# Attention with layer norm on one core: what TensorE does between two bursts of scores

## What is computed

```
q, k, v = x @ wq + bq, x @ wk + bk, x @ wv + bv       # 8 heads of 64
scores  = q @ k.T / 8 + bias[manhattan distance]      # 900 x 900 per head
ctx     = softmax(scores) @ v
out     = layernorm(ctx @ wo + bo + x) * gamma + beta
```

## Time and profile before

| | before |
|---|---|
| median of 3 runs | 3212.4 us (3210.62 to 3213.43) |
| the profiled execution, its own time | 3212.19 us |
| its span, first to last instruction | 3210.2 us |
| mean granted clock of TensorE | 0.993 |
| busy share: TensorE, VectorE, ScalarE, GpSimd | 97%, 81%, 85%, 50% |

### The profile page before, as it was taken

How to read it: one execution, slowest core, us unless ns; L and a number is a source line. 1 busy time by engine, 2 the same in 40 slices (tenths; PEclk the granted TensorE clock), 3 DMA queues, 4 the chain that set the end, 5 groups by cost and what they waited for, 6 DMA issues and landing times. The chain is left out here.

```text
span 3210.2 us, 126640 instructions
## 1 busy us (share of the span) xinstructions
PE 3098.7 (97%) x52264; PEld 2079.8 (65%) x52264; DVE 2610.0 (81%) x5594; ACT 2713.9 (85%) x6903; POOL 1603.4 (50%) x3277
## 2 busy tenths in 40 slices
PE   8899999999999999999999999999999999999986
PEld 5566666666666666666666666666666666666655
DVE  3878879798797978879788797977969788797887
ACT  4988888888888888898888988888888988888885
POOL 1346445465554645546454454645536455464544
PEclk9999999999999999999999999999999999999998
DMA  7332423324233342423324233242332424333231
GB/s 199 73 84 73 94 70 91 77 73 105 62 92 87 76 96 65 96 80 82 85 76 92 71 89 82 73 97 67 95 86 70 98 66 91 86 75 92 65 79 28
DMA packets 523289, 267.80 MB, mean 83 GB/s; under 512 B 329274, under 2 KB 460346, under 8 KB 522590
## 3 DMA queue, kind: packets, MB, share of 16 engines
q1 hardware_dynamic: 375479, 127.82, 18.2%
q10 hardware_dynamic: 147232, 131.88, 14.0%
HBM read 194.10 MB, written 63.44 MB: 80 GB/s over the span
## 5 line engine op out<-in xcount | busy, mean ns | idle before, releaser
L1000 DVE CUSTOM_DVE_ANT_0 prob<-s_ps,window 128x450 f32<-128x450 f32 x1920 | 1107.9, 613 | 441.4 <-PE s_ps L720 441.3
L842 ACT ACTIVATE prob<-prob,own 128x450 f32<-128x450 f32 x1920 | 1265.4, 662 | 142.7 <-DVE own L1000 129.3
L858 ACT ACTIVATE prob<-prob,weight 128x450 f32<-128x450 f32 x1920 | 1173.5, 660 | 47.0 <-POOL weight L1147 44.1
L1016 DVE STREAM_TRANSPOSE prob_t<-prob 128x960 f32<-128x960 f32 x960 | 1125.8, 1173 | 72.7 <-PE pv_ps L740 39.9
L740 PEld LDWEIGHTS pv_ps<-prob_t,values 64*64 64x64 f32 x30720 | 753.6, 133 | 378.0 <-issue 330.9
L720 PE MATMUL s_ps<-k_sb,q_sb 64*32 64x450 f32 x15360 | 853.2, 546 | 38.1 <-DVE own L1000 34.3
L740 PE MATMUL pv_ps<-prob_t,values 64*64 64x120 f32 x30720 | 857.8, 260 | 24.4 <-ACT ctx_sb L868 21.5
L634 PE MATMUL r_ps<-xt,w_sb 128*128 128x450 f32 x3072 | 704.1, 376 | 8.8 <-ACT prob_t L816 3.7
L634 PEld LDWEIGHTS r_ps<-xt,w_sb 128*128 128x128 f32 x3072 | 564.4, 190 | 92.5 <-issue 27.2
L1133 POOL TENSOR_TENSOR lead<-own,other 128x4 f32<-128x4 f32 x480 | 102.1, 213 | 985.0 <-DMA other<-own 984.7
L1147 POOL TENSOR_TENSOR weight<-total,minus_one 128x4 f32<-128x4 f32 x480 | 502.8, 1048 | 37.7
(11 more groups left out here) (63 smaller groups left out, 1488.0 us busy)
## 6 DMA issues: line engine op xcount, KB each, us to landing
w_sb<-w_split ACTq DMA_DIRECT2D x126, 512.0 KB, 4.0
values<-v_dram ACTq DMA_DIRECT2D x256, 240.0 KB, 3.2
other<-own SPq DMA_DIRECT2D x1920, 1.0 KB, 2.2
tokens<-in_x SPq DMA_DIRECT2D x420, 64.0 KB, 3.1
tokens<-in_x SPq DMA_DIRECT2D x109, 240.0 KB, 3.1
out<-tokens SPq DMA_DIRECT2D x105, 240.0 KB, 2.7
v_dram<-stage SPq DMA_DIRECT2D x90, 240.0 KB, 2.8
v_dram<-stage SPq DMA_DIRECT2D x30, 180.0 KB, 2.3
```

Source lines behind the costliest of these rows:

```text
L842: nc.scalar.activation(prob[:, im.unit(u) % RING, head, 0:HALF], prob[:, im.unit(u) % RING, head, 0:HALF], ACT.Exp, scale=-1.0, bias=own[: ...
L858: nc.scalar.activation(prob[:, im.unit(u) % RING, head, 0:HALF], prob[:, im.unit(u) % RING, head, 0:HALF], ACT.Copy, scale=weight[:, s, c: ...
L1000: nc.vector.tensor_tensor_reduce(prob[:, im.unit(u) % RING, head, 0:HALF], s_ps[:, u % 2, head, 0:HALF], window[:, w0:w0 + HALF // GRID, : ...
L1016: nc.vector.transpose(out=prob_t[:, g % 2, v % PER_GROUP, :, :].rearrange("p h k -> p (h k)"), in_=prob[:, im.unit(u) % RING, :, :].rearra ...
```

## The change

Groups have 5 units (three per pair, 12 per image), the ring has 7 units, and a slot holds either one whole group of P x V or up to two whole projections, by a table written out. `x_turned`, the buffer of the transposed new x, lies over a part of `ctx_sb` (the end of pair 2 and the begin of pair 3), which adds two waits to VectorE and one to ScalarE. Eviction times, load times, split times and the order at SyncE change with it.

```diff
-PER_GROUP = 4
+PER_GROUP = 5
-RING = 8
+RING = 7
-PV_UNITS = [4, 8, 12, 16, 20, 24, 28, 32, 34, 38, 42, 46, 50, 54, 58, 62]
-PV_CUT = 8
-SPLIT_UNITS = [0, 0, 4, 6, 8, 11, 14, 17]
-LOAD_X = [22, 24, 28, 32]
+PV_UNITS = [6, 10, 16, 20, 26, 30, 36, 40, 46, 50, 56, 60]
+SPLIT_UNITS = [0, 0, 3, 5, 6, 10, 13, 15]
+LOAD_X = [20, 22, 26, 29]
+X_UNITS = [30, 31, 32, 33, 34, 36, 38, 40]
-FINAL_UNITS = [54, 54, 58, 58, 60, 60, 62, 62]
-FINAL_EVICT = [57, 57, 61, 61, 63, 63, 65, 66]
+FINAL_UNITS = [54, 54, 58, 58, 60, 62, 62, 64]
+FINAL_EVICT = [57, 57, 61, 61, 62, 64, 65, 66]
+def pv_groups(u, last=False):
+    return [g for g, at in enumerate(PV_UNITS) if (min(at, UNITS) if last else at) == u]
+GAPS = {2: pieces(1, (3,)) + [out(0)], 4: [out(1), out(2)], 8: [out(3)] + pieces(2, (0,)), 12: [out(4)] + pieces(2, (1,)),
+        14: [out(5)] + pieces(2, (2,)), 18: [out(6)] + pieces(2, (3,)), 22: [out(7)] + pieces(3, (0,)),
+        24: pieces(3, (1, 2)), 28: pieces(3, (3,)), 32: [value(0), value(1)], 34: [value(2), value(3)],
+        38: [value(4), value(5)], 42: [value(6)] + pieces(4, (0,)), 44: pieces(4, (1, 2)), 48: pieces(4, (3,)),
+        52: [value(7)] + pieces(5, (0,)), 54: pieces(5, (1,)), 58: pieces(5, (2,))}
+SEQUENCE = [item for u in sorted(GAPS) for item in GAPS[u]]
+EVICT = {item: u + (2 if n and item[0] != "out" else 1) for u in GAPS for n, item in enumerate(GAPS[u])}
...
-        x_turned = sb("x_turned", [128, 2, D])
+        x_turned = ctx_flat[:, (PAIRS - 1) * S - 300:(PAIRS - 1) * S - 300 + 2 * D].rearrange("p (i d) -> p i d", i=2)
...
             def body(im, u):                                   (SyncE)
+                for work in im.evicted(u):
+                    if work[0] == "value":
+                        keep_value(im, work[1])
                 if u % 2 and im.live(u + 5):
                     exchange(im, u + 5)
...
-                for work in im.evicted(u - 1):
-                    if work[0] == "value":
-                        keep_value(im, work[1])
...
-                for of, g, j0, j1 in im.parts(u):              (TensorE)
-                    context(of, g, j0, j1)
+                for of, g in im.groups(u):
+                    context(of, g)
                 for work in im.background(u):
-                    work_on(im, work[:-2], *work[-2:])
+                    work_on(im, work)
...
                 if p == 0 and not im.first:                    (ScalarE, keep_context)
-                    act.wait_ge(split_lo, NT * (im.b - 1) + 2 * gi + 2)
+                    act.wait_ge(split_lo, NT * (im.b - 1) + tiles_to(gi))
+                if g == GROUPS - PAIR_GROUPS - 1 and not im.last:
+                    act.wait_ge(x_lo, X_TILES * (im.b + 1))
...
+                if t == 0 and im.first:                        (VectorE, turn_x)
+                    dve.wait_ge(wq_kept, 16 * 2 * PAIRS)
+                elif t == 0:
+                    dve.wait_ge(split_lo, NT * im.b)
...
-                    if X_UNITS[t] - 2 == u and not im.last:    (VectorE, body)
+                    if X_UNITS[t] - 1 == u and not im.last:
```

More of the change, by code:

```diff
@@ L115 @@
 X_TILES = -(-S // XB)
[L116 to L119, removed]
 BANK = {item: n % 2 for n, item in enumerate(SEQUENCE)}
@@ L144, in background @@
 def background(u, first, last):
-    work = [(*item, k0, k1) for item, k0, k1 in STEPS.get(u, []) if wanted(item, first, last)]
+    work = [item for item in GAPS.get(u, []) if wanted(item, first, last)]
     if last:
-        work += [("final", t, 0, KT) for t in range(NT) if FINAL_UNITS[t] == u]
+        work += [("final", t) for t in range(NT) if FINAL_UNITS[t] == u]
     return work
 def order(first, last):
-    return [w[:-2] for u in range(END) for w in background(u, first, last) if w[-1] == steps(w)]
+    return [w for u in range(END) for w in background(u, first, last)]
 def evicted(u, first, last):
@@ L205, in live, with groups @@
         return not (self.first and u < 0) and not (self.last and u >= UNITS)
-    def parts(self, u):
-        before = [] if self.first else [(Before(self), *part) for part in pv_parts(u + UNITS)]
-        return before + [(self, *part) for part in pv_parts(u, self.last) if u < UNITS or self.last]
+    def groups(self, u):
+        before = [] if self.first else [(Before(self), g) for g in pv_groups(u + UNITS)]
+        return before + [(self, g) for g in pv_groups(u, self.last) if u < UNITS or self.last]
     def background(self, u):
@@ L619, in piece @@
                 bank, pair = bank_of(use), im.pair(p)
[L620 to L632, removed]
+                bank_wait(im, use)
+                if im is pro and j == 0:
+                    first_xt_ready(NT - 2)
+                    first_xt_ready(NT - 1)
+                if j == 0 and p == PAIRS and im is not pro:
+                    pe.wait_ge(x_lo, X_TILES * (im.b + 1))
+                if half == 0:
+                    if known(pair):
+                        pe.wait_ge(lo_done[("wk0", "wq0")[kind]], 1)
+                    else:
+                        pe.wait_ge(w_in[kind], 16 * pair)
+                for k in range(KT):
                     for i, (a, c) in enumerate(TERMS):
@@ L694, in work_on @@
                 else:
-                    out_tile(im, work, k0, k1)
+                    out_tile(im, work)
             def scores(im, u):
@@ L914, in body @@
                         stage_value(im, work[1])
-                for of, g, j0, j1 in im.parts(u - 1):
-                    if j1 == BLOCKS:
-                        keep_context(of, g)
+                for of, g in im.groups(u - 1):
+                    keep_context(of, g)
                 if im.live(u + AHEAD):
@@ L1083, in body @@
                 for t in range(X_TILES):
-                    if X_UNITS[t] - 2 == u and not im.last:
+                    if X_UNITS[t] - 1 == u and not im.last:
                         turn_x(im, t)
```

85 lines of the change are left out of this document (36 added, 49 removed).

## The result

| | before | after |
|---|---|---|
| median of 4 runs each | 3212.6 us | 3174.8 us (3168.8 to 3182.1) |
| ratio | | 0.9884 (95% interval 0.9863 to 0.9905) |
| the profiled execution, its own time; its span | 3212.19; 3210.2 | 3174.42; 3172.5 |
| mean granted clock | 0.993 | 0.991 |

What follows compares the result with a forecast made beforehand. TensorE's queue was taken to bound 14 middle images; scores 50.1, P x V 47.8, projections 87.0 and stalls 4.5 us give 189.4 us an image, 5.6 less; 15 x 5.6 = 84 gives 3128 us, range 3095 to 3185.

Steps and rivals of the forecast that it cites:

- Term 1: TensorE's P x V: twelve whole groups of 5 at 3.98 us, 47.8 us per image for 51.1, gain 3.3 us.
- term 2: TensorE's projections merged into 18 slots: 87.0 us per image for 89.4, gain 2.4 us.
- Rival 3: TensorE pays the 0.2 us at every tile shape change, so gains shrink to near nothing: 3205 to 3215 us; chance 0.04.
- Rival 5: TensorE pays a price per key block, at most 0.015 us, saved by 60 fewer blocks: 3114 us; chance 0.02.
- term 3: TensorE's stalls per middle image: 4.5 us after the change, about what stood before (4.4 us).
- SyncE, "I leave 1.5 us": Five loads and three exchanges crowd SyncE's bodies 29 to 33; late exchanges hold ScalarE: 1.5 us of stalls per image.
- The value writes, "nothing, 0.6 us": Value writes moved ahead of SyncE's exchange cost nothing, or their 0.6 us of issue if ScalarE is late.
- `pv_ps`, "1.4 us per image": TensorE's wait for ScalarE to empty this PSUM goes, 1.4 us per image, as groups come at least 4 units apart.
- "1 for what I can't see": Allowance of 1 us of unseen stalls per image, added to 3.5 us of listed ones.
- Rival 1: Uneven slot lengths give thinner covers for ScalarE, adding 3.5 us of stalls per image: 3181 us; chance 0.20.
- Rival 4: TensorE's stalls almost vanish, 1.5 us per image: 3083 us; chance 0.06.
- Rival 2: ScalarE blocks 1.5 us on each whole P x V group, 7.7 us more per image: 3327 us, slower; chance 0.08.

Runs made afterwards that it cites:

- experiment 1: The changed kernel with each tile of new x loaded by one DMA in place of four (tile order differs, values wrong): 3118.5 us.
- experiment 5: The changed kernel with tiles 4 to 7 of the new x loaded in bodies 30, 32, 34, 36 in place of 30 to 33: 3135.9 us.
- experiment 7: The kernel before the change with each tile of new x loaded by one DMA in place of four: 3186.1 us, ratio 0.9918.
- the small norm: The changed kernel with VectorE's statistics, centring and scaling of an output tile over 64 of 512 columns: 3139.8 us.
- experiment 2: The changed kernel with loads of x tiles 3 to 7 at units 28, 30, 32, 34, 36 in place of 29 to 33: 3186.4 us.

## Why the prediction was half right

**Term 1 (P x V) and term 2 (projections) hold.** 3.99 us per group for 3.98, mixed pair 5.42 for 5.4, value pair 5.76 (slot 38: 7.43 less 1.67) for 5.71, two pieces 5.09 for 5.1. Slots without waits sum to 185.3 us for my 184.9 (its 43.4 for eight mixed pairs at 5.4 should be 43.2). The price per burst and column is thus right at 150 columns too, and 60 fewer blocks per image brought no more than that: the 15 blocks of a group take 3.75 us for their columns, and 0.24 is left. By the prediction's estimate, the weight-load rule of the Trainium skill (TensorE: Matmul & The Clock Gate, What overlaps and what doesn't) would have put some 0.2 us into every block, 3 us into a group. This trace disagrees, as the one before did, with its 0.24 us in 15 blocks. Rival 3 falls: the price per burst is 0.24 and not above 0.4. Rival 5 falls too, since the slots without waits sum to more than my figure and not to less. From start to start, no joint between scores and projection costs anything: a burst of scores that nothing delays takes 1.67 us ahead of either.

**The step that failed is term 3, the stalls after:** 4.5 us predicted, 7.8 measured (185.3 to 193.1). A middle image was to fall by 5.6 us and fell by 2.5, 44 us of the missing 46 over the 14: 3.3 an image are these stalls and 0.4 is work, less 0.5 because the mean image before took 195.5 and not the 195.0 of my window. Point by point:

- *SyncE, "I leave 1.5 us".* This is the mis-sized term: by experiment 1 it is 3.5 us (3.8 by the medians), 2.8 of them by the place of the loads alone (experiment 5). I had the right queue in the right bodies, but took 0.6 us per DMA from an exchange, where the loads of the crowded bodies average 0.67 to 0.76, so 21.9 us for 19.4; and I priced the exchange's lateness, not the value write's and not that of the load itself, for which slot 34 waits.
- *The value writes, "nothing, 0.6 us".* Wrong twice. They stand behind whatever loads are still being issued (5.4 us of them in the trace), and ScalarE blocks on them. Moved back, they cost 7.0 us more in a middle image.
- *I set after's loads against nothing:* experiment 7 shows that 2.0 us of the same cost stood in the kernel before, inside my 4.4. What the change added is 1.5.
- *VectorE, "1 us".* 1.7 by the table (2.3 by the medians), but the kernel before had 2.6 of it. The balance of these two is about -0.9, which I did not count.
- *`pv_ps`, "1.4 us per image".* The wait is gone as said, but the earlier trace rows was misread: 10.8 of the 21.5 us lie in the last image, and the 14 middle intervals had 0.6 us each.
- *ScalarE in the singles, "1 us".* Slots 48, 54 and 58 exceed 4.33 by 0.2 us together. Its slack was enough.
- *Ring of 7, `x_turned`.* The ring shows as five waits of VectorE for its own turn, 2.5 us in the whole run; no new wait for `x_turned` shows. A ring of 8 beside groups of five was not run.
- *"1 for what I can't see"* had to hold slot 4, 1.7 us, where a P x V-free pair of output tiles waits for GpSimd's split and ScalarE's eviction at once. In the kernel before slot 4 is 6.46 us and waits for nothing.

The sum of the changes: SyncE +1.5, VectorE -0.9, slot 4 +1.7, the rest (slots 0 and 32, where nothing was tested) +0.6: 2.9, the growth from 4.9 to 7.8. The shares overlap a little, since the causes were taken away one at a time. Slot 4 has the largest of them and stood in no point of my list.

**Ends:** the two half images were to save 5.6 us, with nothing within 5 for the tail; begin and end together saved 3.2.

**Rivals.** Rival 1's time (3181) is nearest, 6 us off, but not by its mechanism. Its sign was scores split by waits in slots 48 to 60 or 6 to 10. The first are the cleanest. Slot 8 does show it (0.9 us an image), but for VectorE, and the small norm takes it away; ScalarE's waits at `ratios` fell from 114.7 to 94.0 us over the span. The stalls sit in the double slots, where two evictions, splits or writes of a kind fall due at once. Rival 4 (3083, stalls of 1.5 us an image) falls with the 7.8. Rival 2 falls: ScalarE waits 45.5 us in all for P x V, 0.24 per group, where it asked for 1.5:

```profile
ACT ratio L811 <- POOL lead L1102: 94.0, 97, 3.6
...
ACT ctx_sb L831 <- PE pv_ps L702: 45.5, 36, 7.5
```

**Open:** what slot 4 would cost with its pair taken apart, how much of slot 32 (0.5 us, GpSimd's split of the new x) is SyncE's, and whether issue or packets hold slot 34.

## What to carry to other kernels

When work is merged into larger bursts, price the burst from start to start, but then list for each helper queue what falls due together: pairs of tiles make pairs of evictions, writes and splits, and a double buffer is full at the third. On a strict queue count every issued DMA of the crowded bodies and ask what short write stands behind them. And take the suspected cost out of the kernel before as well: a cost that both share explains nothing of the difference, however large it is.

## What the runs showed of the hardware

A wait of TensorE can cost more than its length. The windows of experiment 2 around the 3.25 us wait in slot 32 (length, busy time of each engine, granted clock, DMA):

```profile
1516.00:1525.60 9.60, 9.60 (x188) 6.52 (x172) 9.04 (x19) 7.59 (x20) 3.71 (x7) 1.00 0.39 98
1525.60:1528.90 3.30, 0.11 (x1) 0.10 (x1) 0.11 (x1) 2.09 (x6) 2.41 (x5) 1.00 0.46 71
1528.90:1533.10 4.20, 4.14 (x12) 2.75 (x12) 3.48 (x7) 3.24 (x8) 3.40 (x6) 0.66 0.19 28
1533.10:1535.00 1.90, 1.90 (x33) 0.49 (x32) 0.53 (x1) 1.90 (x6) 1.81 (x3) 0.84 0.75 125
```

After 3.3 us with next to no matmul the granted clock was 0.66, a mean of the levels 2.4 and 1.2 GHz, and the value tile took 4.21 us instead of 3.04, the scores behind it 1.99 instead of 1.74: 1.4 us on top of the wait. The image of the kernel after shows no such drop: its window has 1.00. And the issue of one DMA on SyncE's queue is no constant: over the kernel after, its median is 0.59 us in an exchange, 0.64 in a load of x and 0.38 in a value tile's write, with some 0.04 us between two of a row. Single ones last much longer (up to 1.9, 2.1 and 1.7 us), so the groups of the crowded bodies average 0.61 to 0.66 us per DMA in an exchange and 0.67 to 0.76 in a load.
